# TensorE's order from a cycle of positions in place of a list schedule with delays, in a three-layer decoder kernel

## What is computed

```python
# local:  softmax over keys with |i - j| <= 3
scores = where(mask, einsum('bhqd,bhkd->bhqk', q, k) * SCALE, -inf)
# cross:  q from x, k and v from the context (120 keys); no mask
# causal: qkv without bias behind an rms norm; keys up to the query
# feed-forward, with two weights of a softmax over 8 experts
ef  = silu(xf @ up_w.T) @ down_w.T          # 256 -> 1024 -> 256
out = ef * sum(top_2(softmax(xf @ gate_w.T)) / (their sum + 1e-9))
```

## Time and profile before

| | before |
|---|---|
| median of 3 timed runs | 3605.91 us (3600.19, 3605.91, 3607.89) |
| profiled execution | span 3601.5 us; the page gives no other time for it |
| mean granted clock of TensorE | 0.989 |
| busy: TensorE, VectorE, GpSimd, ScalarE | 3488.3, 2764.0, 2507.6, 1715.7 us |
| DMA | 221.54 MB, 62 GB/s |

### The profile page before, as it was taken

How to read it: one execution, slowest core, us unless ns; L and a number is a source line. 1 busy time by engine, 2 the same in 40 slices (tenths; PEclk the granted TensorE clock), 3 DMA queues, 4 the chain that set the end, 5 groups by cost and what they waited for, 6 DMA issues and landing times.

```text
span 3601.5 us, 97036 instructions
## 1 busy us (share of the span) xinstructions
PE 3488.3 (97%) x38789; PEld 2853.8 (79%) x38789; DVE 2764.0 (77%) x6256; ACT 1715.7 (48%) x4049; POOL 2507.6 (70%) x3159
## 2 busy tenths in 40 slices
PE   6699999999999999999999999999999999999998
PEld 5578888888888888888888888888888888888876
DVE  5677787787787787787787877877877877877863
ACT  2345545545545445445545545445445455455443
POOL 5767777777777677677677777777677677677742
PEclk8899999999999999999999999999999999999999
DMA  5111111111121121121121121111111111111100
GB/s 177 48 50 59 61 67 53 66 69 48 67 72 45 67 74 45 67 74 45 67 74 45 67 73 46 67 67 53 67 63 57 67 60 60 67 57 62 67 8 10
DMA packets 87098, 221.54 MB, mean 62 GB/s; under 512 B 8262, under 2 KB 53634, under 8 KB 70274
## 3 DMA queue, kind: packets, MB, share of 16 engines
q1 hardware_dynamic: 86658, 215.34, 16.9%
HBM read 164.92 MB, written 50.39 MB: 60 GB/s over the span
## 4 chain that ended last, share of the span: by engine, by line
PE 93%; DVE 4%; ACT 2%; issue 1%; POOL 0%; DMA 0%; SPq 0%; DVEq 0%; ACTq 0%
PE ps L869 13%; PE ps L860 13%; PE ps L722 11%; PE ps L700 10%; PE ps L839 9%; PE ps L756 8%; PE ps L811 8%; PE ps L788 6%; PE ps L728 5%; PE ps L680 3%; PE ps L780 3%; PE ps L849 2%; DVE held L1355 1%; PE ps L750 1%; ACT rest L1002 1%; DVE nmax_pair L1292 1%
## 5 line engine op out<-in xcount | busy, mean ns | idle before, releaser
L1124 POOL TENSOR_TENSOR chunks<-v_windows,xT 128x560 f32<-128x560 f32 (+1 forms) x384 | 870.8, 2284 | 259.0 <-DVE xT L1267 155.0
L1292 DVE TENSOR_REDUCE nmax_pair<-ps 128x4 f32<-128x480 f32 (+2 forms) x1280 | 776.1, 669 | 167.8 <-PE ps L756 167.5
L1119 POOL TENSOR_TENSOR chunks<-rest,k_windows 128x512 f32<-128x512 f32 (+1 forms) x384 | 552.9, 1455 | 436.8 <-DVE xT L1246 232.6
L969 ACT ACTIVATE prob<-ps 128x256 f32<-128x256 f32 (+2 forms) x1536 | 670.0, 548 | 331.9 <-PE ps L788 331.9
L860 PE MATMUL ps<-xT,w_up 128*128 128x256 f32 x2048 | 483.7, 384 | 0.0
L869 PE MATMUL ps<-w_down,held 128*128 128x256 f32 x2048 | 458.9, 382 | 1.8 <-DVE held L1355 1.6
L869 PEld LDWEIGHTS ps<-w_down,held 128*128 128x128 f32 x2048 | 383.9, 190 | 72.2 <-issue 20.4
L860 PEld LDWEIGHTS ps<-xT,w_up 128*128 128x128 f32 x2048 | 375.7, 191 | 44.7 <-issue 0.9
L1246 DVE TENSOR_REDUCE xT<-chunks 128x32 f32<-128x512 f32 (+1 forms) x384 | 294.0, 766 | 128.0 <-POOL chunks L1119 128.0
L927 ACT COPY xT<-ps 128x512 f32<-128x512 f32 x256 | 149.8, 585 | 489.3 <-PE ps L680 489.2
L1136 POOL TENSOR_SCALAR_AFFINE_SELECT prob<-prob 128x512 f32<-128x512 f32 x512 | 319.5, 655 | 75.7 <-ACT prob L969 75.7
(11 more groups left out here) (146 smaller groups left out, 6086.6 us busy)
## 6 DMA issues: line engine op xcount, KB each, us to landing
k_windows<-passed_on SPq DMA_DIRECT2D x64, 1024.0 KB, 4.6
v_windows<-passed_on SPq DMA_DIRECT2D x64, 1024.0 KB, 5.1
x<-in_x SPq DMA_DIRECT2D x64, 256.0 KB, 2.9
passed_on<-rest SPq DMA_DIRECT2D x64, 256.0 KB, 2.0
passed_on<-held SPq DMA_DIRECT2D x64, 256.0 KB, 2.0
out<-x SPq DMA_DIRECT2D x64, 256.0 KB, 2.1
y<-in_ctx SPq DMA_DIRECT2D x64, 120.0 KB, 2.8
w_up<-in_up SPq DMA_DIRECT2D x1, 1024.0 KB, 8.8
```

The lines of the kernel that those rows point to most:

```text
L969: last = nc.scalar.activation(prob_pair(seq, L, m)[0:keys, :, r, col:col + qs], of_pair, ACT.Exp, scale=SCALE)
L1119: last = nc.gpsimd.tensor_tensor(chunk_of(c).rearrange("p (j d) -> p j d", d=D), q_row, window("k", (b + first) * D, (D, n), (1, D)), ALU. ...
L1124: last = nc.gpsimd.tensor_tensor(chunk_of(c).rearrange("p (h i j) -> p h i j", i=HD, j=WINDOW), window("v", b * D + first * HD, (HD, n), ( ...
L1292: nc.vector.tensor_reduce(nmax[s][:, tb, heads], src, AX_X, ALU.max, negate=True).then_inc(emptied[b], 1)
```

## The change

`DELAY`, `STAY` and `SENIORITY` go. In their place:

- `POSITION` gives each of TensorE's 38 steps a position in periods. Step i of sequence n stands in TensorE's line at n + position. In the middle of the program TensorE takes only the head of the line (and waits if it isn't ready). While the head's position is under FILLING = 6, and in the last 4 periods, it may take any ready step among the first 61: the head if it can, otherwise one that fits the present division, otherwise the first.
- The steps of the other engines are still taken from a sorted list of the ready ones. The key is n plus a due position: the earliest of the followers' due positions plus an entry of `SHIFTED` (76 entries, between -1.542 and 1.0606 periods). Steps of the setup without an entry have 0 on TensorE.
- Scores 0 and 1 of one layer and sequence take the two "prob" buffers as a pair: once one is taken, no other layer or sequence may take the second (`half_way`).
- TensorE's durations and the charges for division in the planner are new (1.73 for 1.63 us for a projection, and so on), and a few of the other engines'.

The instructions that a step issues are not touched. The core of the diff; the other entries of `SHIFTED` and the other durations are left out:

```diff
--- before.py
+++ after.py
@@ -72,21 +72,46 @@
 PLACES = {"lane": LANES, "prob": PROBS, "k_window": 1, "v_window": 1, "chunks": 1}
 
 DIVIDED = {"max": "rows", "scores": "rows", "values": "columns"}
-DIVIDE, REJOIN, CHANGE = 0.33, 0.2, 0.1
-
-STAY = 210.0
-
-SENIORITY = 5.0
-
-DELAY = {("gate", None, "PE"): 55, ("project", 2, "PE"): 2975, ("project_out", 1, "PE"): -85,
-         ("scores", 1, "PE"): -1705, ("scores", 2, "PE"): -110, ("shift", 1, "PE"): -30, ("shift", 2, "PE"): 70,
-         ("turn", 0, "PE"): 25, ("turn", 2, "PE"): 50, ("turn_ctx", None, "PE"): 45, ("up", None, "PE"): 2500,
-         ("values", 1, "PE"): 65, ("gate", None, "ACT"): 30, ("norm", 1, "ACT"): 15, ("norm", 2, "ACT"): 45,
-         ("project", 2, "ACT"): -45, ("turn", 0, "ACT"): 10, ("gate", None, "DVE"): -10, ("max", 1, "DVE"): -100,
-         ("max", 2, "DVE"): 295, ("moments", 0, "DVE"): 10, ("moments", 2, "DVE"): -25,
-         ("moments", 3, "DVE"): 55, ("project_out", 1, "DVE"): 80, ("project_out", 2, "DVE"): 40,
-         ("window_reduce", None, "DVE"): 1295, ("moments", 2, "POOL"): -45, ("norm", 1, "POOL"): -180}
-
+DIVIDE, REJOIN, CHANGE = 0.1, 0.2, 0.11
+
+POSITION = {("turn", (0,)): 0.6553, ("project_rows", ("k",)): 0.7181, ("project_rows", ("v",)): 0.8435, ("turn_ctx",
+    ()): 0.87, ("project_rows", ("q",)): 0.8783, ("project", (1, "k")): 1.5809, ("turn_out", ()): 1.7634,
+    ("project_out", (0,)): 2.026, ("turn", (1,)): 2.2267, ("project", (1, "q")): 2.2449, ("project", (1, "v")):
+    2.3594, ("max", (1, 0)): 2.4515, ("max", (1, 1)): 2.4715, ("shift", (1,)): 2.8781, ("scores", (1, 0)): 2.9805,
+    ("scores", (1, 1)): 2.9813, ("values", (1,)): 3.029, ("project_out", (1,)): 3.2447, ("turn", (2,)): 3.4375,
+    ("project", (2, "k")): 3.4927, ("project", (2, "q")): 3.5203, ("max", (2, 0)): 3.5331, ("project", (2, "v")):
+    3.5335, ("max", (2, 1)): 3.7636, ("max", (2, 2)): 3.7636, ("shift", (2,)): 4.0723, ("scores", (2, 1)): 4.14,
+    ("scores", (2, 0)): 4.2269, ("scores", (2, 2)): 4.3457, ("values", (2,)): 4.5205, ("project_out", (2,)): 4.6965,
+    ("turn", (3,)): 4.9131, ("up", (0,)): 4.9932, ("gate", ()): 5.0258, ("up", (1,)): 5.0937, ("up", (2,)): 5.1683,
+    ("up", (3,)): 5.1737, ("down", ()): 5.3971}
+
...
+    ("window_reduce", (1,), "DVE"): 1.0606, ("window_reduce", (2,), "DVE"): 0.0385, ("window_reduce", (3,), "DVE"):
...
+FILLING, LOOKS = 6, 60
...
-                pe = part("project_rows", (w,), "PE", 1.63, [turned, *before], [("single", ("project_rows", (w,)))])
+                pe = part("project_rows", (w,), "PE", 1.73, [turned, *before], [("single", ("project_rows", (w,)))])
...
-                pe = 0.89 if layer == CROSS else 1.44 if tb == 0 else 1.15
+                pe = 0.95 if layer == CROSS else 1.17 if tb == 0 else 1.05
...
-                a = part(*step, "PE", 1.04, [shifted] + first[0::2],
+                a = part(*step, "PE", 1.1, [shifted] + first[0::2],
...
-        followers, left = defaultdict(list), [0.0] * len(parts)
+        followers = defaultdict(list)
         for i, p in enumerate(parts):
             for a in p.after:
                 followers[at[a]].append(i)
+        due = [0.0] * len(parts)
         for i in reversed(range(len(parts))):
-            left[i] = parts[i].busy + parts[i].lag + max((left[j] for j in followers[i]), default=0.0)
-        delay = [DELAY.get((p.name, p.args[0] if p.name in BY_LAYER else None, p.engine), 0.0) for p in parts]
+            name, args, engine = parts[i][:3]
+            if engine == "PE":
+                due[i] = POSITION.get((name, args), 0.0)
+            else:
+                due[i] = min((due[j] for j in followers[i]), default=6.0) + SHIFTED.get((name, args, engine), 0.0)
         engines = ("PE", "ACT", "DVE", "POOL", "SP")
         self.order = {e: [] for e in engines}
         self.slot, self.before = {}, {}
@@ -285,13 +314,15 @@
         empty = set(range(BANKS))
         last = {}
         divided = None
+        half_way = []
         missing = {(n, i): len(p.after) for n in range(N) for i, p in enumerate(parts)}
         todo = [(n, i) for n in range(N) for i in range(len(parts)) if n == 0 or i >= len(once)]
         ready = {e: [] for e in engines}
 
         def offer(n, i):
-            ready[parts[i].engine].append((SENIORITY * n - left[i] + delay[i], n, i))
-            ready[parts[i].engine].sort()
+            if parts[i].engine != "PE":
+                ready[parts[i].engine].append((n + due[i] + 0.001 * n, n, i))
+                ready[parts[i].engine].sort()
 
         for n, i in todo:
             if not parts[i].after:
@@ -299,7 +330,9 @@
         def whole_half():
             return next((half for half in HALVES if empty.issuperset(half)), None)
 
-        def fits(p):
+        def fits(p, n):
+            if p.name == "scores" and p.args[1] < 2 and half_way and half_way != [(n, p.args[0])]:
+                return False
             wanted = Counter(kind for kind, _ in p.takes)
             return (len(empty) >= wanted["single"] and (not wanted["quad"] or whole_half()) and
                     all(len(free[kind]) >= k for kind, k in wanted.items() if kind in free))
@@ -315,18 +348,19 @@
             empty.difference_update(banks)
             return banks
 
+        line = sorted((n + due[i], n, i) for n, i in todo if parts[i].engine == "PE")
+        ending = line[-1][0] - 4
+
         def next_in_line(e, divided):
-            first = None
-            for entry in ready[e]:
-                if first and entry[0] > first[0] + STAY:
-                    break
-                p = parts[entry[2]]
-                same = e != "PE" or DIVIDED.get(p.name) == divided
-                if (same or not first) and fits(p):
-                    if same:
-                        return entry
-                    first = entry
-            return first
+            if e != "PE":
+                return next((entry for entry in ready[e] if fits(parts[entry[2]], entry[1])), None)
+            filling = line and (line[0][0] < FILLING or line[0][0] > ending)
+            could = [entry for entry in line[:LOOKS + 1 if filling else 1]
+                     if not missing[entry[1:]] and fits(parts[entry[2]], entry[1])]
+            if could[:1] == line[:1]:
+                return could[0] if could else None
+            return next((entry for entry in could if DIVIDED.get(parts[entry[2]].name) == divided),
+                        could[0] if could else None)
 
         idle, events, now = set(engines), {}, 0.0
         while True:
@@ -337,13 +371,15 @@
                 if entry:
                     _, n, i = entry
                     p = parts[i]
-                    ready[e].remove(entry)
+                    (line if e == "PE" else ready[e]).remove(entry)
                     for kind, use in p.takes:
                         place = take(kind)
                         self.slot[kind, n, use] = place
                         if kind in free:
                             self.before[kind, n, use] = last.get((kind, place))
                             last[kind, place] = (n, use)
+                    if e == "PE" and p.name == "scores" and p.args[1] < 2:
+                        half_way = [] if half_way else [(n, p.args[0])]
```

More of the change, by code:

```diff
@@ L155, in sequence_parts @@
         added = [part("norm", (layer,), "POOL", 1.37, [normed])] if layer < CAUSAL else []
-        turned = through("turn", (layer,), 0.4, "ACT", 0.49, [normed])
+        turned = through("turn", (layer,), 0.44, "ACT", 0.49, [normed])
         if layer == LOCAL:
@@ L169, in sequence_parts @@
                 if c == DOTS:
-                    a = part("window_max", (), "DVE", 1.3, reduced[-1:])
+                    a = part("window_max", (), "DVE", 1.68, reduced[-1:])
                     a = part("window_exp", (), "ACT", 0.3, [a])
@@ L191, in sequence_parts @@
             for f, (tb, ms, keys) in enumerate(max_fills(layer, T, C)):
-                pe = 0.89 if layer == CROSS else 1.44 if tb == 0 else 1.15
+                pe = 0.95 if layer == CROSS else 1.17 if tb == 0 else 1.05
                 step = ("max", (layer, f))
                 a = part(*step, "PE", pe, operands, [("quad", step)])
-                last = [part(*step, "DVE", 2.4, [a, *last], (), [("quad", step)])]
+                last = [part(*step, "DVE", 2.28 if layer == CROSS else 2.4, [a, *last], (), [("quad", step)])]
             a = part("round_max", (layer,), "DVE", 0.6, last)
@@ L211, in sequence_parts @@
             halves = [("single", ("values", (layer, m))) for m in range(2)]
-            a = part("values", (layer,), "PE", 1.66 if layer == CROSS else 2.54, [*ready, valued], halves,
+            a = part("values", (layer,), "PE", 1.7 if layer == CROSS else 2.56, [*ready, valued], halves,
                      [("prob", (layer, m)) for m in range(2)])
-            attended = part("normalise", (layer,), "DVE", 2.8, [a], (), halves)
```

(11 more changed lines are left out.)

34 lines of the change are left out of this document (29 added, 5 removed).

## The result

| | before | changed |
|---|---|---|
| median of 15 timed runs | 3606.97 us | 3613.32 us |
| lowest, highest | 3600.19, 3611.71 | 3605.70, 3617.60 |
| ratio to before, 95% interval | | 1.0018 [1.0011, 1.0026] |
| span of the profiled execution | 3601.5 us | 3615.0 us |

The account below looks back on a forecast made before the run. TensorE, busy for 97% of the span, was taken as the bound, with losses in fill and drain. Steady -4, fill -8 and clock -2 summed to -14 us, from 3605.9 to 3592 us; range 3570 to 3612.

Parts of the forecast that it names:

- Steady sum: Steady part, 59 periods: extra visit +0.31 us, lost wait -0.37 us, so -0.06 us a period, -4 us; bounds -22 and +14.
- the wait of L780: Steady part: the causal scores' wait on VectorE's L1355, 0.37 us a period, goes because those scores stand apart.
- the eighth visit: Steady order: TensorE visits the divided array (max, scores, values) eight times a period instead of seven, +0.31 us.
- the second cross max: Steady part: needs the PSUM half that "down" and "turn" leave; margin 0.3 us, no wait taken, 0.3 us a period as bound.
- the DMAs: Setup and DMAs: SyncE's queue keeps its kinds of issues, loads stay bound to the lane's store; 0 us.
- a visit alone costs 0.31 us: Divided array on TensorE: one extra visit lengthens neighbouring steps by 0.31 us together, read from their starts.
- Fill: First 226 us: earlier window reductions give -8 us, matmuls at the higher clock -2 us; bounds -25 and +15.
- Drain: End of the span: order greedy before and after, so 0 us, with bounds -8 and +8.
- Rival 1: Steady part: TensorE's strict order brings a new wait each period, priced at 0.6 us, +21 us, 3627 us; chance 0.13.
- The range: Whole kernel: 3570 us (rival of more gain from the fill) to 3612 us (no fill gain, with the moved wait).

Follow-up runs that it names:

- split_visit: Changed kernel with causal max 0 one place later, behind the v projection, for nine visits a period: period 54.45 us, 3627.75 us (1 run).
- warm_fill: Changed kernel with 76 matmuls of no use ahead of 17 steps of the fill: 3610.89 us, 1.0009 of the kernel before.
- old_drain: Changed kernel with all engines choosing by the rule of the kernel before for the last 4.5 periods: 3598.18 us, 0.9977 of the kernel before.
- warm_drain: Changed kernel with 39 matmuls of no use ahead of ten TensorE steps of the last three sequences: 3607.96 us, 1.0002 of the kernel before.
- merge_visit: Changed kernel with causal scores (2,0) directly behind (2,1), for seven visits a period: period 58.03 us, 3823.85 us (1 run).

## Why the prediction was wrong

- **Steady sum, -0.06 us a period (-4 us).** Right in the period (54.32 for 54.37, a step of 0.05, or 0.02 by the longest median of that order), right that the wait of L780 goes and the eighth visit takes its place, right about what is late next: the second cross max, behind "down". The size over the whole part is -0.3 us, because that wait does occur, in a few periods, with smaller ones beside it. I had put it in the upper bound as a thing of every period or none, and the DMAs at 0; what decides is whether k's windows land late (5.8 us or more), with VectorE waiting for GpSimd's chunks ahead of "down"'s evacuation. That a visit alone costs 0.31 us is not measured; split_visit shows that it costs 0.10 to 0.13 more than a change inside one.
- **Fill, -10 us.** Right sign, -3.9, and the idle time before 226 us is 65.1 us, not near 60. The mechanism shows in part. GpSimd's waits from 50 to 220 us for the v chunks' reductions fell from 13.4 us to 4.9, and those for the softmax in front of them from 21.7 to 11.4; those of the k chunks rose, from 12.7 to 14.5. Before, then changed:

```profile
POOL chunks L1124 <- DVE xT L1267: 21.7, 4, 7.7
...
POOL chunks L1160 <- DVE xT L1303: 11.4, 4, 6.7
...
POOL chunks L1160 <- DVE held L1282: 4.9, 3, 3.1
```

  The third and fourth sequences leave local attention (turn_out) 5.6 and 16.6 us earlier, at 146.0 and 185.9 us, as I had reasoned, but the first two 2.5 and 3.4 us later, and the first "down" belongs to the first. Better clock was part of the gain (0.88 for 0.83 up to the first "down"): 24 us less at half clock, at the tenth that warm_fill shows, are an estimated 2.4 us.
- **Drain, 0.** This is the step that failed. I wrote "Also greedy before and after" and gave nothing, though the diff changes the greedy rule's key from the longest remaining path with hardly any seniority to n + position, the oldest sequence first. With the end of the program in sight the remaining path is what counts: the last sequence must not be left with a chain that nothing covers. The measured term is +17.8 us; old_drain takes it back whole. Up to half of it (9.1 us by warm_drain's trace, 6 by its ratio) is the lower clock behind the idle time, which I had counted in the fill and not in the drain.
- **Rival 1**, a new wait each period, did not come; the loop through the lane never held TensorE up. The slower side came by a mechanism that was none of my rivals.
- **The range** (to 3612) had 8 us for the drain. A part of 175 us in which the deciding rule is replaced wanted bounds of its idle time, 21 us, both ways, and the clock's on top.

In sum: -3.9 - 0.3 + 17.8 = +13.6, with the roundings the 13.5 us between the spans. The medians differ by 6.3 us only. A run's time is 1.8 us more than its span (3616.83 and 3615.0); by that the profiled executions lie 3.6 us below their median (before) and 3.5 above (changed), so the pair of profiles makes the loss look twice as large as it is between typical runs, and I can't say in which part the typical run is better.

What stays open: which of the new priorities gained the 3.9 us in the fill, and why single transfers of k's windows land late.

## What to carry to other kernels

A software pipeline has three parts, and an order that served in its steady period (oldest first, one sequence a period) was wrong for its end, where putting the longest path left first took about 20 us off; price the three apart whenever the rule that orders them is changed. Price an idle gap on TensorE with what may follow it at the lower clock, and not only with its own length: here gaps of 1.90, 2.30 and 2.45 us were followed by steps at half clock, one of 2.38 us and those of 0.37 us were not. In a list executed in order, raising the priority of a step that waits for another engine puts everything behind it at that engine's mercy, and at that of the transfer for which that engine waits.

## What the runs showed that I had not expected

- A wait of 2.30 us in each period of merge_visit cost 3.7 us: the granted clock falls and the next steps are slower (mean 0.97 from 300 to 3300 us). The 0.37 us wait of the kernel before left it at 1.00.
- Taking 41 us of half clock out of the fill gained 4.2 us, 31 us out of the drain 9.1.
- Splitting a visit with a change inside into two visits cost 0.10 to 0.13 us a period.
- A transfer that landed over a microsecond later than usual (5.8 us or more from its issue, for 4.6) reached TensorE over GpSimd and VectorE 30 us later, as a wait of 0.5 to 0.7 us for a bank of PSUM.
